# Attention outputs divided in place instead of by way of transposes, in a decoder layer on one Trainium2 core

## The reference

```python
x = x + _L0_attn_ref(_layernorm(x), ...)           # self layer, causal
x = x + _L0_xattn_ref(_layernorm(x), ctx, ctx, ...)  # cross layer
x = x + _L0_ffn_ref(_layernorm(x), ...)            # experts, not changed here

# the end of either attention
att = jax.nn.softmax(scores, axis=-1)
y = jnp.einsum('bhqk,bhkd->bhqd', att, v)
y = y.transpose(0, 2, 1, 3).reshape(b, t, c)
return y @ Wc                                      # cross layer: @ w_o.T + b_o
```

## Time and profile before

| | |
|---|---|
| median of 3 runs | 1296.25 us (1288.26 to 1298.76) |
| the profiled execution | 1295.45 us, its span 1293.7 us |
| granted TensorE clock, mean over the span | 0.939 |
| self layer, a turn (311.69 to 364.77 us) | 53.1 us |
| cross layer, a turn (710.33 to 771.96 us) | 61.6 us |
| last `ot_l` of attention | ends at 991.7 us |

### The profile page before, as it was taken

The page is one execution under the profiler, slowest core; times in us unless marked ns, Lnnn a source line. Parts: engine busy times, 40 slices in busy tenths (PEclk is TensorE's granted clock), DMA queues, the critical chain, the costliest instruction groups (busy, mean ns, idle before and its releaser), DMA issues. The chain is left out here.

```text
span 1293.7 us, 21922 instructions
## 1 busy us (share of the span) xinstructions
PE 1144.6 (88%) x7616; PEld 683.2 (53%) x7616; DVE 969.7 (75%) x2633; ACT 713.2 (55%) x1429; POOL 530.1 (41%) x728
## 2 busy tenths in 40 slices
PE   5699999999999999999999999999996218999994
PEld 2454545555455554544445454545333217888984
DVE  6678788788888778888888887878861577666551
ACT  6035555545555556676767676666773104565561
POOL 4656375654758443434242424240212003454332
PEclk9669899899999999999999999999999558999997
DMA  5551533515335243342525252415110504454322
GB/s 169 114 116 33 117 85 80 115 35 131 84 99 126 91 115 98 102 100 81 116 66 116 66 115 67 99 54 112 34 42 25 185 4 164 111 112 119 98 26 25
DMA packets 89330, 117.94 MB, mean 91 GB/s; under 512 B 12065, under 2 KB 59105, under 8 KB 89090
## 3 DMA queue, kind: packets, MB, share of 16 engines
q1 hardware_dynamic: 83074, 107.97, 32.5%
q0 software_dynamic: 6144, 8.52, 4.0%
HBM read 48.63 MB, written 16.91 MB: 51 GB/s over the span
## 5 line engine op out<-in xcount | busy, mean ns | idle before, releaser
L785 ACT ACTIVATE probs<-ps_st 128x512 f32<-128x512 f32 (+3 forms) x1024 | 476.5, 518 | 269.6 <-PE ps_st L618 265.6
L638 PE MATMUL ps_p<-kst,qst 63*128 63x512 f32 (+3 forms) x1024 | 383.5, 436 | 9.7 <-DVE mx L895 8.0
L618 PE MATMUL ps_st<-qst,kst 64*128 64x512 f32 (+3 forms) x1024 | 360.1, 419 | 9.2 <-ACT probs L785 8.4
L893 DVE TENSOR_REDUCE mx<-ps_p 128x1 f32<-128x512 f32 x512 | 322.3, 681 | 43.0 <-PE ps_p L638 42.2
L618 PEld LDWEIGHTS ps_st<-qst,kst 64*128 64x128 f32 x1024 | 165.9, 187 | 261.7 <-ACT probs L785 199.9
L895 DVE CUSTOM_DVE_ANT_0 ps_p<-ps_p,tri 128x128 f32<-128x128 f32 (+3 forms) x512 | 238.1, 515 | 13.7 <-PE ps_p L638 12.6
L599 PE MATMUL ps_o<-probs,vals 128*32 128x512 f32 (+3 forms) x2048 | 234.4, 530 | 14.6 <-POOL probs L508 14.6
L638 PEld LDWEIGHTS ps_p<-kst,qst 63*128 63x128 f32 x1024 | 172.5, 189 | 35.3 <-DVE mx L895 15.8
L450 POOL TENSOR_SCALAR lnw<-mv 128x4 f32<-128x4 f32 x24 | 5.1, 211 | 337.1 <-DVE mv L879 337.0
L508 POOL TENSOR_SCALAR_AFFINE_SELECT probs<-probs 128x512 f32<-128x512 f32 x128 | 79.2, 635 | 85.9 <-ACT probs L785 85.5
L1278 PE MATMUL moe_ps_y<-moe_w,moe_hid_h 128*128 128x256 f32 x512 | 94.6, 283 | 0.0
(11 more groups left out here) (224 smaller groups left out, 1893.5 us busy)
## 6 DMA issues: line engine op xcount, KB each, us to landing
qst<-qk_h SPq DMA_DIRECT2D x64, 256.0 KB, 4.7
kst<-qk_h SPq DMA_DIRECT2D x64, 256.0 KB, 4.9
qst<-qk_l SPq DMA_DIRECT2D x32, 256.0 KB, 5.4
kst<-qk_l SPq DMA_DIRECT2D x32, 256.0 KB, 4.9
moe_w1r<-in_w_dram SPq DMA_DIRECT2D x8, 1024.0 KB, 5.0
moe_w2r<-in_w_dram SPq DMA_DIRECT2D x8, 1024.0 KB, 9.9
xin<-in_x_dram SPq DMA_DIRECT2D x8, 512.0 KB, 4.1
xres<-in_x_dram SPq DMA_DIRECT2D x8, 512.0 KB, 3.9
```

Of the source, the lines that this page charges most:

```text
L618: last = nc.tensor.matmul(out, kst[rows, t % 2, pair, kt * P:(kt + 1) * P], qst[rows, t % 2, pair, lo:S], start=True, stop=not masked)
L638: last = nc.tensor.matmul(ps_p1[:, i % 3, 0:keys], qst[rows, t % 2, pair, qt * P:(qt + 1) * P], kst[rows, t % 2, pair, 0:keys], start=True ...
L785: nc.scalar.activation(probs[:, kt, j, 0:n], ps_st[:, i % 2, 0:n], ACT.Exp, scale=float(DH) ** -0.5).then_inc(exp_done, 1)
L893: nc.vector.tensor_reduce(mx[:, g % 2, at:at + 1], bank, AX.X, ALU.max).then_inc(max_done, 1)
```

## The change

Two groups now share one tile, and the division is made where the outputs lie, head by row and query by column, without the way through `og`, `ocomp` and `ot`.

- `vals` gets 48 columns for each pair of heads: 16 values of the even group's head, 16 ones, 16 values of the odd group's head. The 32 columns from 0 give values in rows 0 to 15 and the denominator sixteen times in rows 16 to 31; those from 16 give denominators first, then values. The weights are reordered on the host to fit.
- After the even group ACT copies `ps_o` twice, scaled by a column of `half_of` (one in one half of each 32 rows, zero in the other): the values to `num`, the denominators to `den`. After the odd group DVE adds the other halves with two scalar_tensor_tensor. PE's first `pv` waits for `o_even` or `o_odd` instead of `o_raw`.
- `divide` (once for two groups, slot 13 after them): DVE shuffles `den` by sixteen rows to `moved` and takes its reciprocal, 128x512; `num` times `moved` is DVE's in the self layer, POOL's in the cross layer.
- `high` (slot 15): ACT copies `num` to `ot_h`. `low` (slot 17): `num` less `ot_h` is `ot_l`, by DVE in the self layer, by POOL in the cross layer. `y` waits for it.
- `num`, `den` and `moved` are the memory of `oraw` and of the two halves of `ocomp`. `half_of` is made from `ident` by two reductions at the start.

```diff
-VW = DH + 1
-VROW = H * VW + 16
+VB = 3 * DH
+VROW = PAIRS * VB
...
-M_KINDS = ("xt", "qk", "v", "mt", "og", "ot", "y", "xt3", "lg", "bo")
+M_KINDS = ("xt", "qk", "v", "mt", "y", "xt3", "lg", "bo")
...
-        put(16 * (g + 1) + 15, "og", g)
+        if g % 2:
+            put(16 * (g + 1) + 13, "divide", g // 2)
+            put(16 * (g + 1) + 15, "high", g // 2)
+            put(16 * (g + 1) + 17, "low", g // 2)
...
-        put(after + 3, "ot", t, 0)
-        put(after + 19, "ot", t, 1)
...
+        XN = KT * B
+
+        def lowered(engine, n):
+
+            if n <= XN:
+                engine.wait_ge(o_low, n)
+            else:
+                engine.wait_ge(x_low, n - XN)
...
+                    elif kind == "divide" and s[1] >= XN:
+                        n = s[1] - XN
+                        pool.wait_ge(x_moved, n + 1)
+                        nc.gpsimd.tensor_tensor(out=num, in0=num, in1=moved, op=ALU.mult).then_inc(x_divided, 1)
+                    elif kind == "low" and s[1] >= XN:
+                        n = s[1]
+                        pool.wait_ge(o_high, n + 1)
+                        nc.gpsimd.tensor_tensor(out=ot_l[:, n % KT, :], in0=num, in1=ot_h[:, n % KT, :].bitcast(F32),
+                                                op=ALU.subtract).then_inc(x_low, 1)
...
-                                pe.wait_ge(o_raw, g)
+                                if g % 2:
+                                    pe.wait_ge(o_even, (g + 1) // 2)
+                                else:
+                                    pe.wait_ge(o_odd, g // 2)
...
-                        at = VW * (GH * (g % GROUPS) + j)
+                        at = VB * (GH * (g % GROUPS // 2) + j) + DH * (g % 2)
...
-                        evicted(pe, ("ot", t, 1))
+                        lowered(pe, KT * (t + 1))
...
-                elif kind == "pv" and s[2:] == (TT - 1, GH - 1):
+                elif kind == "pv" and s[1] % 2 == 0 and s[2:] == (TT - 1, GH - 1):
...
+                        lowered(act, g // 2)
+                    nc.scalar.activation(num, ps_o[:, :], ACT.Copy, scale=half_of[:, 0:1])
+                    nc.scalar.activation(den, ps_o[:, :], ACT.Copy, scale=half_of[:, 1:2]).then_inc(o_even, 1)
+                elif kind == "high":
+                    n = s[1]
+                    if n < XN:
+                        act.wait_ge(o_divided, n + 1)
+                    else:
+                        act.wait_ge(x_divided, n - XN + 1)
+                    if n >= KT:
+                        act.wait_ge(m_ready, M[("y", n // KT - 1, 1)] + 1)
+                    nc.scalar.activation(ot_h[:, n % KT, :], num, ACT.Copy).then_inc(o_high, 1)
...
+                    elif kind == "divide":
+                        n = s[1]
+                        dve.wait_ge(pv_done, 2 * n + 2)
+                        dve.wait_ge(o_even, n + 1)
+                        nc.vector.scalar_tensor_tensor(out=num, in0=ps_o[:, :], scalar=half_of[:, 1:2], in1=num, op0=ALU.mult, op1=ALU.add)
+                        nc.vector.scalar_tensor_tensor(out=den, in0=ps_o[:, :], scalar=half_of[:, 0:1], in1=den, op0=ALU.mult,
+                                                       op1=ALU.add).then_inc(o_odd, 1)
+                        dve.wait_ge(o_odd, n + 1)
+                        link(nc.vector.stream_shuffle(moved, den, [i ^ 16 for i in range(32)]))
+                        if n >= XN:
+                            nc.vector.reciprocal(moved, moved).then_inc(x_moved, 1)
+                            continue
+                        link(nc.vector.reciprocal(moved, moved))
+                        nc.vector.tensor_tensor(out=num, in0=num, in1=moved, op=ALU.mult).then_inc(o_divided, 1)
+                    elif kind == "low" and s[1] < XN:
+                        n = s[1]
+                        dve.wait_ge(o_high, n + 1)
+                        nc.vector.tensor_tensor(out=ot_l[:, n % KT, :], in0=num, in1=ot_h[:, n % KT, :].bitcast(F32),
+                                                op=ALU.subtract).then_inc(o_low, 1)
...
-                    elif kind == "og":
-                        g = s[1]
...
-                        link(nc.vector.reciprocal(rec[:, g % 2, :], view[:, :, DH]))
```

More of the change, by code:

```diff
@@ L182, in attention @@
         ocomp = sb("ocomp", [P, TT, C], F32)
[L183 removed]
+        half_of = sb("half_of", [P, 2], F32)
+        half_max = sb("half_max", [P, 32], F32)
         ot_h = sb("ot_h", [P, KT, S], F32R)
@@ L212, in attention @@
         wc_raw = room[:, 6144:6656]
+        num, den, moved = oraw[:, :], ocomp[:, 0:2, :].rearrange("p a c -> p (a c)"), ocomp[:, 2:4, :].rearrange("p a c -> p (a c)")
         rope2 = ocomp[:, :, :].rearrange("p (a b) c -> p a (b c)", a=2)
@@ L797, in step @@
                         nc.scalar.activation(xt_h[:, s[2], :], bank, ACT.Copy).then_inc(h_done, 1)
-                    elif kind == "ot":
-                        nc.scalar.activation(ot_h[:, s[2], :], bank, ACT.Copy).then_inc(h_done, 1)
                     elif kind == "xt3":
@@ L903, in run @@
                         dve.wait_ge(h_done, HI[s] + 1)
-                    if kind in ("xt", "ot"):
-                        hi, lo = (xt_h, xt_l) if kind == "xt" else (ot_h, ot_l)
-                        nc.vector.tensor_tensor(out=lo[:, s[2], :], in0=bank, in1=hi[:, s[2], :].bitcast(F32),
+                    if kind == "xt":
+                        nc.vector.tensor_tensor(out=xt_l[:, s[2], :], in0=bank, in1=xt_h[:, s[2], :].bitcast(F32),
                                                 op=ALU.subtract).then_inc(m_free, 1)
```

59 lines of the change are left out of this document (28 added, 31 removed).

## The result

The changed kernel takes 1482.11 us, median of 4 runs (1477.24 to 1486.36). The kernel before took 1293.88 us beside it. The ratio is 1.1455, with a 95% interval of 1.1392 to 1.1519: 188 us slower. The forecast was 1424, with a range of 1360 to 1490. The direction and the range held; the sum was 58 us short.

What follows compares the result with a forecast made beforehand. The prediction took PE's order of work as the bound of both layers. Cross 54, self 56, end of attention 5 and clock 13 made 128 us on 1295.5: 1424 us, range 1360 to 1490.

Steps and rivals of the forecast that it cites:

- PE as the bound, and the transposes: PE's order of work sets both layers' time; removing 96 transpose steps saves 62.8 us, 2.0 us a pair of groups.
- Durations: Prices of DVE's new operations: reciprocal 3.45 us, each scalar_tensor_tensor 0.75, shuffle 0.74, multiply and subtract 1.1 each in self.
- Wait A: PE waits at slot 14 for o_odd behind DVE's max and two operations: 2.3 us a pair, both layers.
- Wait B: PE stops for p1 maxima while DVE does shuffle and reciprocal: 2.5 us a pair in cross, 3.4 in self.
- C: Cross layer: ACT stands at high behind POOL's multiply, delaying exps; PE is back 0.8 us later a pair.
- All pauses together: PE's pauses a pair, less waits already there: cross 2.3 + 2.5 + 0.8 - 0.2; self 2.3 + 3.4 + 0.3 - 0.5.
- The clock: Four more dips of PE's granted clock, all in the self layer, about 3.2 us each: 13 us.
- End of attention: The tail after the last group grows from 4.3 to 9.5 us: +5 us.
- The clock behind every stall: Rival: clock falls to 1.2 GHz behind every stall; 1462 us with self-layer dips, 1513 with cross too; chance 0.14.
- Overlap of the waits: Rival: new waits overlap existing ones, each layer runs at DVE's pace; 77 us more, 1372 us; chance 0.13.
- VectorE and GpSimd hold each other up: Rival: in the self layer multiply and subtract take 1.67 us each beside POOL; +26, 1450 us; chance 0.08.
- The two cases with a short reciprocal: Rivals: reciprocal of 0.69 us, about 1300 us, chance 0.06; slot 14 wait gone too, 1238 us, chance 0.05.

Runs made afterwards that it cites:

- e9_nolump: Changed kernel with the two ps_o operations at slot 11, a cheap pass replacing the reciprocal (outputs not divided), high and low at slots 21 and 23: 1349.0 us.
- e8_lump: Kernel before plus one 128x512 reciprocal with unused result on VectorE, in one piece at slot 13 behind every second group: 1389.4 us.
- e4_warm: Changed kernel plus unused PE matmuls, two ahead of the wait for o_odd and two ahead of the p1 tile of slot 17: 1467.4 us.
- e1_cheap: Changed kernel with the 32 reciprocals replaced by a one-pass tensor_scalar of the same size, outputs not divided: 1416.1 us.
- e6_all: Changed kernel with the two ps_o operations at slot 11, the reciprocal in four pieces at slots 13 to 16, high and low at 21 and 23: 1428.9 us.
- e12_poolself: e6_all with the multiply and low on GpSimd in the self layer too: 1438.1 us.
- e10_spread: Kernel before plus one unused 128x512 reciprocal behind every second group, in eight pieces of 64 columns at slots 9 to 16: 1337.7 us.
- the fills: Two runs adding unused PE matmuls to the changed kernel: e4_warm, 1467.4 us, and one with three ahead of the wait for o_odd only, 1496.0 us.

## Why the prediction was right in its range and short in its sum

*PE as the bound, and the transposes.* Right, but of little weight. The 384 matmuls are gone. A saving can be seen only where the long pauses are gone: in the cross layer of e9_nolump PE is busy for 58.1 us a turn, against 60.6, which is 2.5 of the 3.9 us.

*Durations.* Right for the most part. The reciprocal took 3.353 us for a forecast of 3.45: between 32 and 512 elements it is (3.353 - 0.353) / 480 = 6.25 ns an element, for 6.4. The Trainium skill (VectorE: DVE Perf Modes, the section on modes) states a repeat count of 8, from which I had the estimate of 4.3 us. The measurement decides against this estimate. The scalar_tensor_tensor took 0.74 (0.75), the shuffle 0.74, multiply and low 0.69 in the median, for which I had put 1.1; that is 0.8 us a pair too much in the self layer. The term of the copies was a little low: with a scale read for each partition they take 0.69 us, not 0.6.

*Wait A.* Right in place and kind, and somewhat small in size: the two rows of waits above are 84.4 us in 30 times, 2.8 us each, for 2.3; 2.60 us in the cross layer at 865.42, up to 3.7 in the self layer.

*Wait B.* This step failed as a term to be added to A. I put 2.5 and 3.4 us a pair for it. In the changed kernel the waits behind a maximum are 22.9 us in 24 times, about 1 us each, in the self layer, and hardly there in the cross layer. At 865.42 PE comes out of A before the reciprocal has begun, but with the clock at 0.55 it needs 7 us for the next 32 matmuls, and by then the lump is over. Where the clock stayed at 1.00 behind A, waits B and C are there: 1.22 and 1.43 us at 798.78 and 801.70. Alone, the lump costs about what I put, 3.0 us a pair in e8_lump, in the cross layer for the most part by way of another bank.

*All pauses together.* I had 5.4 us (cross) and 5.5 us (self) a pair for A, B, C and low, less what was there already, 174 us in all. PE's idle time grew by 4.05 and 3.8 us a pair, 126 us: 48 us too much in the sum.

*The clock.* This is the term that was mis-sized. I put 13 us for it, four dips in the self layer. The step that failed is "At the end of the cross layer PE was busy for 4.8 of 8 us and kept 1.00. I count four more dips". That row was read as if no pause of the change could bring a fall in the cross layer, and as if few would in the self layer. The change makes single pauses of 2.1 to 3.7 us. The clock was then at the lower level for 27 us of a self turn and 7 us of a cross turn, and PE's matmuls became longer by 10.6 and 4.7 us a turn, 123 us. With 174 - 48 + 123 - 63 the sum is 186, without the end of attention, and the span's growth is 184.9; eight times the middle turns is a little more than the layers grew.

What the lower clock cost in time is less than the 123 us. In the self layer e4_warm shows at least 4.2 us a turn, 34 us. In the cross layer the one place compared above took 7.54 us at the full clock and 7.53 us at 0.55. Measured turns were 68.1 and 70.5 us where I had 61 and 68. So about three quarters of the miss are in the self layer, and at least 4.2 of the 7.1 us a turn there are the clock's. The rest in the cross layer fits the waits that were put too small, A with 2.6 to 3.15 us for 2.3 and C with 1.15 for 0.8. That the range held is in part luck: in PE's bookkeeping the pauses were 48 us too many and the slower matmuls 110 us too few.

*End of attention.* Right: from the first operation on `ps_o` at 1165.66 to the end of the last low at 1174.56 are 8.9 us, for 9.5.

*The rivals.* The clock behind every stall (1462 for the self layer, 1513 for both) is near to what happened in kind, with falls in both layers, but not behind every pause and at smaller pauses than I had in it. That 1482 lies between its two values says little. Overlap of the waits (1372) is true of A and B, but by way of the slow clock: slow matmuls stand where B and C would. That VectorE and GpSimd hold each other up hardly shows in the changed kernel: multiply and low at 0.69 us in the median, longest 1.10 and 1.97 us. The rule of the Trainium skill (SBUF — State Buffer, "Who interferes with whom") may be behind those two longest ones; as a price for this change it does not matter. Other versions show more of it: in e1_cheap and e9_nolump, with a short pass in place of the reciprocal, the multiply takes 0.96 us in the median and 1.64 at the longest. The two cases with a short reciprocal had no ground, since it took 3.35 us; yet e9_nolump shows that they too were priced too low: with a pass of some 0.45 us in its place and A gone, the kernel took 1349 us, not 1238.

*What stays open.* Why the self turn of e9_nolump is 6 us over the kernel before, and why the clock stays at 0.81 in the self layer of e6_all and at 0.77 in that of e12_poolself, where PE has only three or four pauses over 1.5 us in four turns. VectorE's sum as the bound of the self layer was my second theory and fell twice (e10_spread, e12_poolself). A chain of short pieces without room between them is what is left, argued and not shown. Nor did a run price the clock in the cross layer by itself, since the fills brought a wait there. Why the clock fell behind five of the eight pauses of the cross layer and not, or only later, behind the other three is open too.

## What to carry to other kernels

Where PE is fed through two or three banks, the longest single piece in the queue of a feeding engine counts before its sum does: the same reciprocal cost 97 us in one piece and 44 us in eight, and in the changed kernel, moved to another feeding engine, it cost as much as ever (1497 against 1482 us). Two pauses close together are not to be added, and taking one of them away shows the other; take both away before judging either. Look at the clock behind a pause of PE before you price it, and then ask whether a faster PE would only wait longer. Here 2.6 us of standing once brought 7 us at nearly half speed; in the self layer the lower clock cost at least 4.2 us a turn, and in the cross layer the same stretch took as long with it as without. PE's busy time grew with the clock's fall (123 us), and that is no measure of what the fall cost.

## What the hardware showed that I had not expected

One pause of PE of 2.6 to 3.5 us can be enough, in a layer that otherwise runs at 1.00, to put the granted clock to 0.50 for most of the next 6 to 7 us, although PE is busy throughout these (6.98 of 7.00 us at 0.55). It isn't always: in the changed kernel the clock stayed at 1.00 in the 7 us behind three of eight such pauses. Matmuls with unused results, 7.6 us a turn, made the self turn 4.2 us shorter by keeping the clock at 0.96 in place of 0.80. A PE at half the clock can lose nothing: 32 matmuls took 6.98 us of 7.00 at 0.55 and 4.85 us of 7.00 at 1.00, and the next tile came after 7.53 and 7.54 us. The reciprocal on VectorE takes 6.25 ns for each further element between 128x32 and 128x512, 3.353 us for the latter. An exp and a ln in turn on ScalarE cost a table load of 1.28 us each time, twice the pass of 0.63 us itself. A scale read for each partition makes a copy of 128x512 on ScalarE 0.69 us instead of 0.60.
